# An attention pipeline re-cut into rounds of two steps: matmul pairs in runs of two, three and three

## The chip, the cores and the metric

The kernel runs on one core of a Trainium2 chip. The metric is device time in microseconds, from launch to end. TensorE (PE) multiplies matrices into PSUM (8 banks of 128 x 512 float32), VectorE (DVE), ScalarE (ACT) and GpSimd (POOL) work on elements, SyncE (SP) starts DMAs. The engines run their own instruction streams in order and meet at semaphores.

## The reference

A batch of 4 sequences of 1024 positions with 128 channels goes through a time-mixing layer (projections and a decaying scan), and then through a cell of six attention nodes. The six nodes are nearly all of the time:

```python
for c in range(NUM_NOD):
    nsrc = min(c + 1, MAX_PREV)
    snode = c - nsrc
    eq, ek, ev = (lind + nsrc - 1, lind, lind + nsrc // 2)
    in_q, in_k, in_v = (c - 1, snode, snode + nsrc // 2)
    q = ew[c, 0] * (nodes[in_q] @ We[eq] + be[eq])
    k = ew[c, 1] * (nodes[in_k] @ We[ek] + be[ek])
    v = ew[c, 2] * (nodes[in_v] @ We[ev] + be[ev])
    o = _mha(q, k, v, Wq[c], Wk[c], Wv[c], Wo[c])      # 8 heads of 16 channels, softmax over 1024 keys
    nodes[c] = act_w[c] * o + q
    lind += nsrc
```

## The kernel before

Node and batch entry make a **unit**: 6 x 4 = 24 units, one after the other. A unit is 4 **groups** (4 heads x 512 queries), and a group is 8 **steps** of 128 keys, so there are 768 steps (`STEPS`), 32 per unit (`UC`). In step s TensorE does, for each of the 4 heads of the group:

- a **score** matmul (L540, 50 rows x 128 keys, 512 queries), which writes one of three PSUM banks (`ring`); ScalarE turns it into the exponential in one of 10 slots of `e_ring` (L853). The row maximum is subtracted inside the matmul, by two extra rows of `q_aug`, so the maxima must be known in advance.
- a **maxima** matmul (L566) for the group that comes `LOOKAHEAD` = 14 steps later: 128 queries x 512 keys, into half of one of two double banks (`wide`). Two of them make a **tile** of 128 queries x 1024 keys, which VectorE reduces in one instruction (L1133). There are two tiles in a step, 1536 in all.

Score and maxima matmul use different halves of the array's rows (heads of other parity) and run side by side. Such two are called a **pair** here. After two pairs stands half of a **block**: the exponentials of the step before times the values (L588, four matmuls in the four column groups of the array, 256 query columns each, into the bank `context`). A step is thus pair, pair, half block, pair, pair, half block.

Every unit needs eight **projections** of 128 x 512, which are single matmuls in full width, at fixed steps r = s mod 32: two each for keys (`KH_AT`, L463), output (`OUT_AT`, L491 and L496), values (`V_AT`, L482) and queries (`QH_AT`, L471). In such a step the projection stands in the place of the first half block, and the whole block (512 columns) comes at the step's end. Projections take `ring` banks. ScalarE empties them (L745, L764, L778), for values VectorE does (L998).

Every 8 steps a group of maxima is complete (`finished`); at the start of that step VectorE makes two splits and a transpose of them (L1138, L1142, L1151), and SyncE writes them to DRAM and loads them back into `q_aug`. Every 8 steps ScalarE empties `context` (L868). Once a unit, VectorE takes the reciprocal of the denominators (L1074).

Ahead of step 0 come the time mixing and 14 steps with maxima alone, with filler matmuls (L426); the last 14 steps have no maxima. In the first units some of the time mixing (`MIX_AT`) still runs beside the attention.

Everything is ordered by hand: each engine's program walks over the same steps, and the places of all else are tables of step numbers.

## Time and profile before

| | |
|---|---|
| median of 3 runs | 2265.6 us (2264.27, 2265.6, 2288.34) |
| profiled execution | 2265.8 us, of which the span of the trace 2264.0 us |
| TensorE busy | 2231.4 us (99%) |
| VectorE busy | 2055.1 us (91%) |
| ScalarE busy | 1829.0 us (81%) |
| GpSimd busy | 529.3 us (23%) |
| granted TensorE clock | 0.998 of full |

Times on a line of a trace are start and duration in microseconds from the start of the span. A line with x2 or more merges neighbours: its duration runs from the start of the first to the end of the last. PEld is the weight load that belongs to a matmul, PE the matmul itself. "idle before <-" names how long the engine stood and what let it go.

### The profile page before, as it was taken

To read this page: it belongs to the slowest core of one execution; us is meant where nothing else is said; L and a number is where in the kernel's file an instruction comes from. 1 tells how busy PE (TensorE), PEld (TensorE's weight loads), DVE (VectorE), ACT (ScalarE), POOL (GpSimd) and SP (SyncE) were. 2 spreads that over 40 slices of the span, in tenths; PEclk is the share of its full clock that TensorE was granted. 3 is DMA by queue.
4 is the path that set the end of the run, shared out by engine and by line. 5 is a ranking of instruction groups with operands and counts; after the bars stand their busy time and mean duration, and the time that the engine had idled before them with its cause. 6 is when DMAs were issued, how large, how long until landed. Compare 5 with 4: busy or idle time off the path is not lost.

```text
span 2264.0 us, 46280 instructions
## 1 busy us (share of the span) xinstructions
PE 2231.4 (99%) x17991; PEld 848.7 (37%) x17991; DVE 2055.1 (91%) x2254; ACT 1829.0 (81%) x3431; POOL 529.3 (23%) x667
## 2 busy tenths in 40 slices
PE   7999999999999999999999999999999999999997
PEld 3533333333333333333333333333333333333332
DVE  6989999999999999999998999999999999989995
ACT  4277888888888888888888888888888888888886
POOL 4431230221312202202112112122022022321313
PEclk9999999999999999999999999999999999999999
DMA  4230332422313314224223233133132242241301
GB/s 126 64 72 25 81 71 49 89 64 66 80 46 91 71 33 92 60 61 85 64 57 81 55 69 80 36 78 80 34 82 62 49 85 54 61 95 42 74 25 53
DMA packets 87546, 149.55 MB, mean 66 GB/s; under 512 B 35147, under 2 KB 49951, under 8 KB 87327
## 3 DMA queue, kind: packets, MB, share of 16 engines
q0 software_dynamic: 28224, 94.13, 19.2%
q1 hardware_dynamic: 59102, 52.46, 9.2%
q8 instruction: 142, 2.33, 0.4%
q14 instruction: 78, 0.63, 0.1%
HBM read 42.36 MB, written 14.91 MB: 25 GB/s over the span
## 4 chain that ended last, share of the span: by engine, by line
PE 95%; DVE 2%; issue 1%; ACT 1%; SPq 0%; POOL 0%; DMA 0%; POOLq 0%; ACTq 0%; DVEq 0%
PE ring L540 43%; PE context L588 36%; PE ring L482 2%; PE ring L471 2%; PE ring L463 2%; PE ring L491 2%; PE ring L496 2%; PE wide L566 2%; DVE max_neg L1133 1%; PE context L426 1%; PE ring L369 0%; ACT e_ring L853 0%; PE ring L394 0%; PE ring L391 0%; PE ring L405 0%
## 5 line engine op out<-in xcount | busy, mean ns | idle before, releaser
L1133 DVE TENSOR_REDUCE max_neg<-wide 128x1 f32<-128x1024 f32 x1536 | 1850.4, 1220 | 142.2 <-PE wide L566 136.4
L853 ACT ACTIVATE e_ring<-ring 128x512 f32<-128x512 f32 x3052 | 1658.2, 597 | 286.6 <-PE ring L540 147.6
L566 PE MATMUL wide<-k_aug,q_aug 48*128 48x512 f32 x3072 | 1121.3, 444 | 2.3 <-DVE max_neg L1133 1.4
L540 PE MATMUL ring<-q_aug,k_aug 50*128 50x512 f32 x3052 | 1114.1, 444 | 0.0
L588 PE MATMUL context<-e_ring,v_aug 128*32 128x256 f32 (+1 forms) x10664 | 938.4, 424 | 1.8 <-ACT raw L868 1.6
L540 PEld LDWEIGHTS ring<-q_aug,k_aug 50*128 50x128 f32 x3052 | 455.7, 184 | 749.7 <-ACT e_ring L853 550.3
L566 PEld LDWEIGHTS wide<-k_aug,q_aug 48*128 48x128 f32 x3072 | 457.9, 184 | 12.9 <-issue 6.5
L588 PEld LDWEIGHTS context<-e_ring,v_aug 128*32 128x32 f32 x10664 | 209.9, 107 | 477.0 <-issue 340.9
L342 POOL DMA_DIRECT2D src<-node_dram x40 | 22.9, 572 | 633.2 <-PE ring L482 633.2
L1233 POOL CAST q_part<-q_part 128x512 fp32r<-128x512 f32 x46 | 28.1, 611 | 476.7 <-ACT q_part L778 302.0
L312 POOL DMA_DIRECT2D q_aug<-q_part x138 | 72.1, 522 | 126.3 <-PE ring L540 126.3
L1190 POOL TENSOR_TENSOR rstd<-vareps,neg_half 128x4 f32<-128x4 f32 x24 | 26.9, 1122 | 219.6 <-DVE vareps L897 219.4
L1259 POOL TENSOR_TENSOR ctxT<-ctxT,rden_bc 128x1024 f32<-128x1024 f32 x23 | 54.7, 2377 | 92.3 <-DMA rden_bc<-rden_dram 92.3
L312 POOL DMA_DIRECT2D k_aug<-k_part x138 | 70.0, 514 | 15.1 <-PE ring L540 9.8
L745 ACT ACTIVATE node_ring<-ring,col 128x512 f32<-128x512 f32 x47 | 32.3, 688 | 48.7 <-PE ring L496 40.8
L1235 POOL TENSOR_TENSOR k_part<-k_part 128x512 f32<-128x512 f32 x47 | 60.3, 1283 | 4.9 <-DVE src L902 1.2
L1235 POOL TENSOR_TENSOR q_part<-q_part 128x512 f32<-128x512 f32 x47 | 60.2, 1281 | 4.0 <-POOL k_part L1235 0.2
L868 ACT ACTIVATE raw<-context 128x512 f32<-128x512 f32 x96 | 58.0, 604 | 0.8 <-PE context L588 0.8
L471 PE MATMUL ring<-node_ring,w_q 128*128 128x512 f32 x92 | 51.8, 645 | 0.1
L491 PE MATMUL ring<-node_ring,w_edge_q 128*128 128x512 f32 x92 | 51.8, 644 | 0.0
L1233 POOL CAST k_part<-k_part 128x512 fp32r<-128x512 f32 x46 | 28.3, 615 | 82.9 <-ACT k_part L764 47.5
L496 PE MATMUL ring<-ctxT,w_o 128*128 128x512 f32 x92 | 47.0, 592 | 0.0
(241 smaller groups left out, 890.8 us busy)
## 6 DMA issues: line engine op xcount, KB each, us to landing
q_aug<-q_part POOLq DMA_DIRECT2D x138, 256.0 KB, 4.5
k_aug<-k_part POOLq DMA_DIRECT2D x138, 256.0 KB, 7.1
src<-node_dram POOLq DMA_DIRECT2D x40, 512.0 KB, 7.2
ctxT<-raw SPq DMA_DIRECT2D x380, 32.0 KB, 2.0
rden_bc<-rden_dram SPq DMA_DIRECT2D x23, 512.0 KB
node_dram<-node_ring SPq DMA_DIRECT2D x16, 512.0 KB, 2.9
...
```

The costliest lines, as they stand in the source:

```text
L312: e.dma_start(aug[first + slot:first + SPLIT:len(slots), u % 2, :, :], part[parity:P:2, slots[slot], :]).then_inc(signal, DMA)
L471: e.matmul(bk[:, :], w_q[:, c, :], node_ring[:, b, c % 2, half_of(hf)], start=True, stop=True).then_inc(p_qh, 1)
L491: e.matmul(bk[:, :], w_edge_q[:, c, :], node_ring[:, b, c % 2, half_of(hf)], start=True, stop=False)
L496: e.matmul(bk[:, :], w_o[:, c, :], ctxT[:, half_of(hf)], start=False, stop=True).then_inc(p_o, 1)
L540: e.matmul(bk[:, :], k_aug[first:first + AUG, u % 2, h // 2, chunk * P:(chunk + 1) * P].bitcast(F32R), q_aug[first:first + AUG, u % 2, h / ...
L566: done = e.matmul(wide[w % 2][:, half_of(kh)], q_aug[first:first + SPLIT, u % 2, h // 2, q0:q0 + P].bitcast(F32R), k_aug[first:first + SPL ...
L588: done = e.matmul(bank[CTX_BANK][j * VW:(j + 1) * VW, columns], v_aug[:, u % 2, chunk, hg * HG + j, :], e_ring[:, (HG * z + order_of(z).in ...
L853: e.activation(e_ring[:, n % E_SLOTS, :], bank[where["st", n]][:, :], ACT.Exp, scale=EXP_SCALE).then_inc(a_exp, 1)
L868: e.activation(raw[:, G % 2, :], bank[CTX_BANK][:, :], ACT.Copy).then_inc(a_cv, 1)
L1133: e.tensor_reduce(max_neg[:, G % 2, row:row + 1], wide[w % 2][:, :], AX_X, ALU.max, negate=True).then_inc(v_mx, 1)
L1233: step(e.tensor_copy(high.bitcast(F32R), x))
L1235: signal(e.tensor_tensor(x, x, high, ALU.subtract), signal_to)
```

## The change

Steps are now taken in **rounds** of two (s even, s + 1). The eight pairs of a round stand in runs of two, three and three instead of four runs of two, and three blocks stand between them instead of four half blocks:

- a round without a projection: 2 pairs, half block (second half of step s - 2), 3 pairs, whole block (step s - 1), 3 pairs, half block (first half of step s);
- with a projection, and no middle form: the same, with the projection between the third run and the last half block. This is so where a group begins (s a multiple of 8);
- the **middle form**, in the other rounds with one projection (s mod 8 = 4): 2 pairs, two half blocks in a row, 3 pairs, the projection alone, 3 pairs, two half blocks in a row.

With it go these: the two double banks for the maxima become a ring of four single banks (`MAX_BANKS`), of which projections now take the next one in turn as well; each maxima matmul waits for its own bank and signals for itself; from tile 88 on (`SPLIT_FROM`) every second tile is reduced in two instructions of 512 columns, and so is every tile whose two banks aren't neighbours (`in_halves`: 955 of the 1536 tiles by the tables of the changed kernel). The halves are joined by a minimum when a group is complete, one more small VectorE instruction. ScalarE waits for a free `e_ring` slot once in a step, before its third exponential, and not twice. `LOOKAHEAD` is 12. The projections for queries move by a step, the turning of a final node stands in one round, and the last projection of all is cut in two halves.

By the tables of the changed kernel there are 378 rounds: 193 without a projection, 95 with projections at the end, and 90 of the middle form (23 with keys, 23 with output, 23 with values, 21 with queries).

```diff
--- before.py
+++ after.py
-LOOKAHEAD = 14
+LOOKAHEAD = 12
 E_SLOTS = 10
+MAX_BANKS = 4
...
-        wide = [ctx.enter_context(nc.psum_tensor(f"wide{i}", [P, S], F32)) for i in range(2)]
+        wide = ctx.enter_context(nc.psum_tensor("wide", [P, MAX_BANKS, BANK], F32))
         context = ctx.enter_context(nc.psum_tensor("context", [P, BANK], F32))
-        bank = ([t[:, :] for t in ring] + [t[:, k * BANK:(k + 1) * BANK] for t in wide for k in range(2)] + [context[:, :]])
-        WIDE_BANKS, CTX_BANK = ((3, 4), (5, 6)), 7
+        bank = ([t[:, :] for t in ring] + [wide[:, k, :] for k in range(MAX_BANKS)] + [context[:, :]])
+        MAX_BANK0, CTX_BANK = 3, 7
+        LAST_DEN_BANK, LAST_FILL_BANK = 3, 5
...
-        KH_AT, OUT_AT, TURN_AT, V_AT, QH_AT = (5, 9), (13, 17), (18, 19), (21, 25), (30, UC + 1)
+        K_AT, OUT_AT, TURN_AT, V_AT, Q_AT = (5, 9), (13, 17), 19, (21, 25), (29, UC + 1)
...
+        def products(s):
+
+            u, r = divmod(s, UC)
+            nxt, prev = u + 1, u - 1
+            found = []
+            if 1 <= nxt < UNITS:
+                found += [("k", nxt, hf) for hf in range(2) if r == K_AT[hf]]
+                found += [("v", nxt, hf) for hf in range(2) if r == V_AT[hf]]
+            for unit in (nxt, nxt + 1):
+                if 1 <= unit < UNITS:
+                    found += [("q", unit, hf) for hf in range(2) if s == q_steps(unit)[0][hf]]
+            if 0 <= prev < LAST:
+                found += [("out", prev, hf) for hf in range(2) if r == OUT_AT[hf]]
+                if CELLS[prev][0] == NODES - 1 and r == TURN_AT:
+                    found += [("turn", prev, hf) for hf in range(2)]
+            return found
...
+        SPLIT_FROM = 2 * (UC + LOOKAHEAD)
+
+        def in_middle(s):
+
+            kinds = [kind for kind, _, _ in products(s + 1)]
+            return kinds in (["k"], ["v"], ["q"], ["out"]) and s % NCH != 0
+
+        MAX_BANK_OF, taken = [], 0
+        for s in range(-LOOKAHEAD, ALONE):
+            for k in range(HG):
+                MAX_BANK_OF.append(MAX_BANK0 + taken % MAX_BANKS)
+                taken += 1
+                if s > 0 and s % 2 == 1 and k == (0 if in_middle(s - 1) else HG - 1):
+                    taken += len(products(s))
+
+        def in_halves(w):
+
+            return w >= SPLIT_FROM and w % 2 == 0 or MAX_BANK_OF[2 * w] + 1 != MAX_BANK_OF[2 * w + 1]
+
+        MAXIMA_UP_TO = []
+        for w in range(GROUPS * TILES):
+            before = MAXIMA_UP_TO[-1] if w else 0
+            MAXIMA_UP_TO += [before + 1, before + 2] if in_halves(w) else [before + 1, before + 1]
...
-            def maxima(w, kh):
+            def maxima(h):
+                w, kh = divmod(h, 2)
                 G, t = divmod(w, TILES)
                 u, g = divmod(G, GPU)
                 hg, qh = divmod(g, NHALF)
                 hj, qt = max_tile(t)
-                h = hg * HG + hj
-                first = (h % 2) * ROWS
+                head = hg * HG + hj
+                first = (head % 2) * ROWS
                 q0 = qh * BANK + qt * P
-                if kh == 0:
-                    if w >= 2:
-                        e.wait_ge(v_mx, w - 1)
-                    else:
-                        for i in WIDE_BANKS[w]:
-                            free_bank(i)
+                i = next_max_bank()
+                bk = free_bank(i)
+                freed[i] = (v_mx, MAXIMA_UP_TO[h])
                 if t == 0 and g == 0 and kh == 0 and u > 0:
                     e.wait_ge(d_q, DMA * Q_MOVES * u)
                     e.wait_ge(d_k, DMA * K_MOVES * u)
                 if u == 0 and qh == 0 and t % (2 * CPB) == 0 and kh == 0:
-                    pair = h // 2
+                    pair = head // 2
                     e.wait_ge(d_q0[pair], DMA * Q_MOVES)
                     e.wait_ge(d_k0[pair], DMA * K_MOVES)
-                done = e.matmul(wide[w % 2][:, half_of(kh)], q_aug[first:first + SPLIT, u % 2, h // 2, q0:q0 + P].bitcast(F32R),
-                                k_aug[first:first + SPLIT, u % 2, h // 2, half_of(kh)].bitcast(F32R), start=True, stop=True)
-                if kh == 1:
-                    done.then_inc(p_mx, 1)
+                e.matmul(bk[:, :], q_aug[first:first + SPLIT, u % 2, head // 2, q0:q0 + P].bitcast(F32R),
+                         k_aug[first:first + SPLIT, u % 2, head // 2, half_of(kh)].bitcast(F32R), start=True, stop=True
+                         ).then_inc(p_mx, 1)
...
+            def pair(s, k):
+                scores(s, k)
+                h = HG * (s + LOOKAHEAD) + k
+                if h < 2 * GROUPS * TILES:
+                    maxima(h)
+
+            def product(kind, unit, hf):
+                make = {"k": head_k, "q": head_q, "v": project_v, "out": project_out, "turn": final_turn}[kind]
+                make(unit, hf, next_max_bank())
...
+            for s in range(0, ALONE, 2):
+                pair(s, 0)
+                pair(s, 1)
+                middle = in_middle(s)
+                if s > 0:
+                    weighted(s - 2, second_half, False, True)
+                if middle:
+                    weighted(s - 1, first_half, True, False)
+                pair(s, 2)
+                pair(s, 3)
+                pair(s + 1, 0)
+                if middle:
+                    for kind, unit, hf in products(s + 1):
+                        product(kind, unit, hf)
+                elif s > 0:
+                    weighted(s - 1, whole, True, True)
+                mix_at(s)
+                pair(s + 1, 1)
+                pair(s + 1, 2)
+                pair(s + 1, 3)
+                if middle:
+                    weighted(s - 1, second_half, False, True)
+                else:
+                    for kind, unit, hf in products(s + 1):
+                        product(kind, unit, hf)
+                weighted(s, first_half, True, False)
+                mix_at(s + 1)
...
-                        if n >= E_SLOTS and (n - E_SLOTS) % HG in (0, 2):
-                            e.wait_ge(p_ctx, (n - E_SLOTS) // HG + 1)
...
+                if n >= E_SLOTS and (n - E_SLOTS) % HG == 0:
+                    e.wait_ge(p_ctx, (n - E_SLOTS) // HG + 1)
...
+            for s in range(0, ALONE, 2):
+                for k in range(HG):
+                    exponential(s, k)
+                exponential(s + 1, 0)
+                if s > 0 and s % NCH == 0:
+                    evict_context(s // NCH - 1)
+                if in_middle(s):
+                    for kind, unit, hf in products(s + 1):
+                        evict(kind, unit, hf)
+                mix_at(s)
+                for k in range(1, HG):
+                    exponential(s + 1, k)
+                if not in_middle(s):
+                    for kind, unit, hf in products(s + 1):
+                        evict(kind, unit, hf)
+                mix_at(s + 1)
...
+                first, second = (MAX_BANK_OF[2 * w + kh] - MAX_BANK0 for kh in range(2))
                 if t == 0 and G >= 2:
                     e.wait_ge(v_cmb, G - 1)
-                e.wait_ge(p_mx, w + 1)
-                e.tensor_reduce(max_neg[:, G % 2, row:row + 1], wide[w % 2][:, :], AX_X, ALU.max, negate=True).then_inc(v_mx, 1)
+                if in_halves(w):
+                    for kh, b in enumerate((first, second)):
+                        e.wait_ge(p_mx, 2 * w + kh + 1)
+                        e.tensor_reduce(max_neg[:, G % 2, kh, row:row + 1], wide[:, b, :], AX_X, ALU.max, negate=True).then_inc(v_mx, 1)
+                else:
+                    e.wait_ge(p_mx, 2 * w + 2)
+                    e.tensor_reduce(max_neg[:, G % 2, :, row], wide[:, first:second + 1, :], AX_X, ALU.max, negate=True
+                                    ).then_inc(v_mx, 1)
 
             def split_high(G):
-                e.wait_ge(v_mx, TILES * (G + 1))
-                both = max_neg[:, G % 2, :].rearrange("p (o t) -> p o t", o=2)
-                step(e.tensor_tensor(max_part[:, G % 2, :, 0, :].bitcast(F32R), both, both, ALU.max))
+                e.wait_ge(v_mx, MAXIMA_UP_TO[2 * TILES * (G + 1) - 1])
+                one, two = (max_neg[:, G % 2, kh, :].rearrange("p (o t) -> p o t", o=2) for kh in range(2))
+                e.tensor_tensor(max_all[:, G % 2, :, :], one, two, ALU.min)
+                step(e.tensor_tensor(max_part[:, G % 2, :, 0, :].bitcast(F32R), one, two, ALU.min))
...
+                    if half == 1 and s >= 0:
+                        for odd in (s, s + 1):
+                            if odd % 2 == 1 and in_middle(odd - 1) == (odd != s):
+                                for kind, unit, hf in products(odd):
+                                    if kind == "v":
+                                        evict_v(unit, hf)
```

On TensorE, the two steps with a projection for keys, before, from the half block ahead of that projection's step on (L540 and L566 are a pair, L463 the projection, L588 the block):

```order
L588 MATMUL context<-e_ring,v_aug 32x256 x4
L540 MATMUL ring<-q_aug,k_aug 128x512
L566 MATMUL wide<-k_aug,q_aug 128x512
L540 MATMUL ring<-q_aug,k_aug 128x512
L566 MATMUL wide<-k_aug,q_aug 128x512
L463 MATMUL ring<-src,w_k_fold 128x512
L540 MATMUL ring<-q_aug,k_aug 128x512
L566 MATMUL wide<-k_aug,q_aug 128x512
L540 MATMUL ring<-q_aug,k_aug 128x512
L566 MATMUL wide<-k_aug,q_aug 128x512
L588 MATMUL context<-e_ring,v_aug 32x512 x4
```

The same place in the changed kernel, a round of the middle form (L607 and L631 are a pair, L514 the projection, L652 the block), from its first block on; a third pair and a row like the first follow:

```order
L652 MATMUL context<-e_ring,v_aug 32x256 x8
L607 MATMUL ring<-q_aug,k_aug 128x512
L631 MATMUL wide<-k_aug,q_aug 128x512
L607 MATMUL ring<-q_aug,k_aug 128x512
L631 MATMUL wide<-k_aug,q_aug 128x512
L607 MATMUL ring<-q_aug,k_aug 128x512
L631 MATMUL wide<-k_aug,q_aug 128x512
L514 MATMUL wide<-src,w_k_fold 128x512
L607 MATMUL ring<-q_aug,k_aug 128x512
L631 MATMUL wide<-k_aug,q_aug 128x512
L607 MATMUL ring<-q_aug,k_aug 128x512
L631 MATMUL wide<-k_aug,q_aug 128x512
```

The projection has moved from a `ring` bank into a `wide` bank, and its neighbours on both sides are three pairs.

On VectorE, from one projection for values to the next maxima group, before:

```order
L998 TENSOR_TENSOR v_aug<-ring,v_bias 128x32x16 [waits d_bias_in,p_v,p_ctx]
L1133 TENSOR_REDUCE max_neg<-wide 128x1 [waits p_mx]
L1138 TENSOR_TENSOR max_part<-max_neg 128x2x8 [waits v_mx]
L1142 TENSOR_TENSOR max_part<-max_neg,max_part 128x2x8 [waits v_own]
L1151 STREAM_TRANSPOSE max_turn<-max_part 128x32 [waits v_cmb,d_rows0]
L1133 TENSOR_REDUCE max_neg<-wide 128x1 [waits p_mx,v_cmb]
L1133 TENSOR_REDUCE max_neg<-wide 128x1 [waits p_mx] x15
```

The same engine at the start of a round of the middle form with a projection for values, in the changed kernel (L1254 reduces 512 columns, L1257 a whole tile, L1102 is the old L998):

```order
L1263 TENSOR_TENSOR max_all<-max_neg 128x16 [waits v_mx]
L1264 TENSOR_TENSOR max_part<-max_neg 128x2x8
L1268 TENSOR_TENSOR max_part<-max_all,max_part 128x2x8 [waits v_own]
L1276 STREAM_TRANSPOSE max_turn<-max_part 128x32 [waits v_cmb,d_rows1]
L1254 TENSOR_REDUCE max_neg<-wide 128x1 [waits p_mx,v_cmb]
L1254 TENSOR_REDUCE max_neg<-wide 128x1 [waits p_mx]
L1257 TENSOR_REDUCE max_neg<-wide 128x2 [waits p_mx]
L1102 TENSOR_TENSOR v_aug<-wide,v_bias 128x32x16 [waits d_bias_in,p_v,p_ctx]
L1254 TENSOR_REDUCE max_neg<-wide 128x1 [waits p_mx] x20
```

The four small instructions of a finished group now stand ahead of the tiles of a round that has a projection in its middle; before, they stood in a step without one.

## Rows read from the trace of the kernel before

**Rows 1.** The page: busy us, share of the span, instructions

```profile
PE 2231.4 (99%) x17991; PEld 848.7 (37%) x17991; DVE 2055.1 (91%) x2254; ACT 1829.0 (81%) x3431; POOL 529.3 (23%) x667
```

**Rows 2.** Timeline of TensorE and its weight loads: one half of a step

```profile
1873.48 0.49 PE L540 MATMUL ring<-q_aug,k_aug 50*128 50x512 f32 x1
...
1873.59 0.19 PEld L540 LDWEIGHTS ring<-q_aug,k_aug 50*128 50x128 f32 x1
...
1873.82 0.39 PE L540 MATMUL ring<-q_aug,k_aug 50*128 50x512 f32 x1
...
1874.14 0.64 PE L588 MATMUL context<-e_ring,v_aug 128*32 128x256 f32 x8
...
1874.71 0.49 PE L540 MATMUL ring<-q_aug,k_aug 50*128 50x512 f32 x1
```

**Rows 3.** The same timeline, all engines, at a projection and a finished group

```profile
1877.83 1.16 PE L482 MATMUL ring<-w_v_fold,src 128*128 128x128 f32 x8
...
1878.92 0.50 PE L540 MATMUL ring<-q_aug,k_aug 50*128 50x512 f32 x1
...
1879.11 0.68 DVE L998 TENSOR_TENSOR v_aug<-ring,v_bias 128x512 f32<-128x512 f32 x1
1879.26 0.39 PE L540 MATMUL ring<-q_aug,k_aug 50*128 50x512 f32 x1
...
1879.51 1.09 ACT L853 ACTIVATE e_ring<-ring 128x512 f32<-128x512 f32 x2 [0.43 <-PE ring L540]
1879.58 1.06 PE L588 MATMUL context<-e_ring,v_aug 128*32 128x512 f32 x8
1879.72 1.23 DVE L1133 TENSOR_REDUCE max_neg<-wide 128x1 f32<-128x1024 f32 x1
...
1880.57 0.50 PE L540 MATMUL ring<-q_aug,k_aug 50*128 50x512 f32 x1
...
1881.60 3.46 DVE L1133 TENSOR_REDUCE max_neg<-wide 128x1 f32<-128x1024 f32 x3
```

**Rows 4.** The chain that ended last: fillers and maxima before step 0, a projection

```profile
98.87 0.66 PE wide L566 x2
99.53 0.63 PE context L426 x2
...
1030.04 1.05 PE ring L463 x2
```

**Rows 5.** Timeline of TensorE: a projection for the output

```profile
1052.50 1.12 PE L491 MATMUL ring<-node_ring,w_edge_q 128*128 128x512 f32 x2
...
1054.41 0.50 PE L540 MATMUL ring<-q_aug,k_aug 50*128 50x512 f32 x1
```

**Rows 6.** Timeline of ScalarE: the context is emptied, once a group

```profile
1877.50 0.60 ACT L868 ACTIVATE raw<-context 128x512 f32<-128x512 f32 x1
...
1899.04 0.60 ACT L868 ACTIVATE raw<-context 128x512 f32<-128x512 f32 x1
```

**Rows 7.** Timeline of VectorE and TensorE: a maxima bank that is late

```profile
1045.68 3.46 DVE L1133 TENSOR_REDUCE max_neg<-wide 128x1 f32<-128x1024 f32 x3
...
1046.93 0.49 PE L566 MATMUL wide<-k_aug,q_aug 48*128 48x512 f32 x1 [0.51 <-DVE max_neg L1133]
```

**Rows 8.** Timeline of VectorE: the reciprocal of a unit

```profile
1027.56 0.54 DVE L1074 RECIPROCAL rden_pack<-den_pack 128x64 f32<-128x64 f32 x1
1028.02 3.42 DVE L1133 TENSOR_REDUCE max_neg<-wide 128x1 f32<-128x1024 f32 x3
```

**Rows 9.** Timeline of TensorE: blocks in the last steps, which have no maxima

```profile
2220.20 1.06 PE L588 MATMUL context<-e_ring,v_aug 128*32 128x512 f32 x8
...
2222.25 1.06 PE L588 MATMUL context<-e_ring,v_aug 128*32 128x512 f32 x8
```

**Rows 10.** Timeline of the end: last projection, its statistics

```profile
2252.68 1.10 PE L515 MATMUL ring<-raw,w_last 128*128 128x512 f32 x2 [1.69 <-DVE raw L1026]
...
2255.26 0.89 DVE L888 BATCH_NORM_STATS2 stats<-ring 128x6 f32<-128x128 f32 x4 [0.23 <-PE ring L369]
```

282 lines of the change are left out of this document (147 added, 135 removed), and 2 rows, old and new, of the table MIX_AT.

## The prediction

> **What bounds the kernel now.** I read the page first: TensorE is busy 99% of the span, VectorE 91%, ScalarE 81% [rows 1]. Then the timeline inside a step, to see what TensorE's time is made of. A pair starts 0.34 us after the pair ahead of it, the half block 0.32 after the second pair, the next pair 0.57 after the half block: 1.23 for half a step, 4.92 for two steps [rows 2]. Nothing in it waits. A whole block takes 0.99, only 0.42 more than a half one, a projection 1.05, for values 1.09 and for the output 1.91 [rows 3 to 5]. Two steps with a projection take 2.46 + 2 x 0.66 + 1.05 + 0.99 = 5.82 (values 5.86, output 6.68). A group with one projection for values and one for queries comes to 6 x 2.46 + 3.40 + 3.36 = 21.52, and the trace has 21.54 from one emptying of the context to the next [rows 6]. So TensorE's own order explains the time, and the others fit in beside it.
>
> **What the new order takes off TensorE.** The first pair of a run costs more than the second: its row is 0.49 long against 0.39, because its weights load in the open, while the second pair's load begins 0.11 after the first one's start, in its shadow [rows 2]. So a pair inside a run is worth 0.34 - 0.11 = 0.23. The trace has no run of three; its third pair costs from 0.23 (like the second without the exposed load) to 0.34 (the whole distance). I take 0.23, since the second pair's load already lies under the first pair. A run of two is 0.66, a run of three 0.34 + 0.23 + 0.32 = 0.89. Two half blocks in a row I take as one whole block.
>
> - No projection: 0.66 + 0.57 + 0.89 + 0.99 + 0.89 + 0.57 = 4.57, which is 0.35 less.
> - Projection at the end: 5.62, 0.20 less.
> - Middle form: 0.66 + 0.99 + 0.89 + 1.05 + 0.89 + 0.99 = 5.47, 0.35 less.
>
> If nothing waited, that would be 193 x 0.35 + 95 x 0.20 + 90 x 0.35 = 118 us. Most of it is not to be had.
>
> The Trainium skill speaks against the cheap third pair: "TensorE: Matmul & The Clock Gate", The mechanism, says that a weight load overlaps matmuls in flight only where the row groups differ. Here both row groups are at work and the load still begins 0.11 after the pair, so the trace differs from the rule; by the rule the third pair would be 0.34.
>
> **VectorE's share.** Reductions in a row stand (3.46 - 1.23) / 2 = 1.12 apart [rows 3]. Halves of 512 columns aren't in the trace. The nearest is the value projection's emptying, 512 columns, after which the next reduction starts 0.61 later [rows 3]; from below, half of 1.12 is 0.56. I take 0.59, so a tile in two costs 1.18, and a round with two such tiles 4.60, with four (44 of the rounds without projection) 4.72. VectorE is now as long as TensorE's 4.57. In rounds without a projection I take 4.65: 4.60 from VectorE, and some 0.05 because the fifth score of a round needs the bank of the second. ScalarE starts 0.59 after a run's first pair, its exponentials stand 1.09 - 0.60 = 0.49 apart [rows 3], so the second ends at 0.59 + 0.49 + 0.60 = 1.68, and the fifth pair's weights would load at 1.69. Rounds with the projection at the end: 5.65.
>
> **The middle form, step by step.** A finished group adds 1.88 - 1.12 = 0.76 between two reductions [rows 3]; the new minimum is a fourth such instruction (0 to 0.25 by a third of that), I take 0.10, together 0.86. All groups finish ahead of a round of the middle form. In the round before, the fifth tile half can't be reduced before 3.12 + 0.59 = 3.71, so the last tile starts at 3.71 + 0.03 + 0.59 = 4.33, and the first half of the new round at 4.33 + 1.12 + 0.86 - 4.61 = 1.70 after its start. The second follows at 2.29. The projection takes the bank of the second pair. A whole tile gives its bank back 1.25 after the start of its reduction (1045.68 to 1046.93) [rows 7], a half 0.54 sooner, 0.71. So the projection starts at 3.00 and not at 2.54: **0.46 lost**. Behind it, the whole tile (start 2.88) frees the next bank at 4.13, where TensorE would be at 4.05; the eighth pair needs the fifth one's bank, free at 2.88 + 1.12 + 0.71 = 4.71, just in time, but its load is then in the open (0.1). The last two blocks end at 6.14. ScalarE's seventh exponential waits for a slot that only the first of them frees (5.14 + 0.64 + 0.09), ends at 6.5, and the next round's second pair waits 0.15 for it. Sum 6.29 for keys and queries, where the two steps took 5.82.
>
> - Queries: +0.47, 21 times: 10.
> - Keys: the reciprocal stands just ahead, 0.46 more [rows 8] that used to be hidden behind TensorE. +0.93, 23 times: 21.
> - Output: 1.91 hides the rest, but not the late start: 3.00 + 1.91 + 0.89 + 0.99 + 0.15 = 6.94 against 6.68. +0.26, 23 times: 6.
> - Values: VectorE empties them 1.28 after their start (1877.83 to 1879.11) [rows 3], at 4.28, ahead of the fifth pair's half, which starts at 4.89 and frees the bank at 5.60. The eighth pair waits 0.9. 5.60 + 0.43 + 0.99 + 0.15 = 7.17 against 5.86. +1.31, 23 times: 30.
>
> Together +67 us.
>
> **The rest.** Two steps fewer ahead of step 0 save 2 x 2 x (0.66 + 0.63) = 5.2 [rows 4]; in their stead two of the last steps, 2.05 each [rows 9], become two at 2.33: 4.6 saved in all, 0 to 6. The last projection in halves: from its matmul to the statistics there are 2.58 [rows 10], three operations of which the later half is on the path; I take 1, at most 1.3. SyncE: rows of maxima go out four steps ahead of their use, not six, over 9 us, for a store and a load that take about 6 by the spacing that they have now; no wait. GpSimd's splits and moves keep their steps within one, and it is busy 23%.
>
> **Sum.** -193 x 0.27 = -52, +3 for the 44 with four split tiles, -95 x 0.17 = -16, +67, -4.6, -1: **-4 us**, from the profiled 2265.8 (the median is 2265.6) to **2262 us**. Its own range, with 0.1 us a round either way in 90 rounds and half of that in the others, is 2244 to 2280. A measurement of this kernel can tell about 1%, 23 us.
>
> **Rivals.**
>
> 1. *The middle form doesn't wait* (faster). If the finished group's small instructions and the first halves are done by 2.54, rounds of the middle form cost 5.47 + 0.15, 90 x 0.2 saved in place of 67 lost: 2262 - 85 = 2177. With half of the waits gone: 2220. For it: only VectorE's 0.46 stands between the two, and a late last tile in front makes all of it. Against: the bank follows from the tables, and a late bank already costs TensorE 0.51 once before [rows 7]. Chance 0.25.
>
> 2. *Halves are dear* (slower). If halves in a row stand further apart than 0.60, VectorE sets the rounds without projection. Each 0.01 above costs 140 x 0.04 + 44 x 0.08 + 90 x 0.02 = 11 us; from 0.62 to 0.63 the change is slower by 1%, at the 0.69 of a short reduction standing alone (1.23 - 0.54) it would be 2360. For it: each half waits for a semaphore of its own. Against: the 0.61 after the value projection. Chance 0.17. The Trainium skill, "VectorE: DVE Perf Modes", The TRN2 errata, gives 120 cycles beside the elements for a PSUM source: two halves would cost 0.125 more than a whole, 0.66 each, and by that the time would be near 2330; for the whole it gives 1.19, where the trace has 1.12.
>
> 3. *The third pair costs 0.34* (slower). Rounds without projection are then 4.79 + 0.03, those with one at the end 5.84, the middle form about 0.15 shorter in its waits than it is longer in its pairs: 193 x 0.17 + 95 x 0.19 - 13 = +38, 2300. It decides in every run of three. Chance 0.12.
>
> The forecast itself has 0.46. From these: faster by over 1% (under 2243) 0.27, within 1% 0.49, slower 0.24. The range that should hold 8 in 10 cuts the far end of rival 1 and of rival 2: 2195 to 2310.
>
> **What would show it.** In a round without projection the starts of pairs read 0, 0.34, 1.23, 1.57, 1.80, 3.12, and the round is 4.6 to 4.7 long. Halves of reductions follow at 0.59. In rounds of the middle form TensorE stands about 0.46 ahead of the projection, released by VectorE, and 0.9 ahead of the eighth pair behind values; the four groups of a unit, by their emptyings of the context, take about 21.8, 21.9, 23.1 and 21.3 us from its start on (before, by the sums above, 22.4 in the two that have an output projection and 21.5 in the others). If TensorE is still 99% busy in the middle form, the forecast is wrong, to the fast side.

## The result, and the profile after

The changed kernel takes 2412.2 us (median of 4 runs, 2407.4 to 2418.3) beside 2265.9 for the kernel before: ratio 1.062, 95% interval 1.055 to 1.069. The forecast was 2262, its range ended at 2310.

The page of the kernel after, its first part (engine: busy us, share, instructions), the granted clock and the DMA share in 40 slices, and the lines of the chain:

```profile
PE 2273.9 (94%) x17213; PEld 957.0 (40%) x17213; DVE 2077.8 (86%) x3307; ACT 1789.6 (74%) x3432; POOL 529.6 (22%) x667
...
PEclk9989999999999999999999989999999999899899
DMA  4130331331412323313403223223134133132201
...
PE context L652 21%; PE ring L607 21%; DVE max_neg L1257 10%; DMA rows_dram<-max_turn 9%; DVE max_neg L1254 9%; PE wide L631 6%; PE wide L522 2%; PE wide L533 2%; DMA q_aug<-rows_dram 2%; PE wide L514 2%; PE wide L542 1%; PE wide L547 1%; PE context L477 1%; DVE max_part L1268 1%; DVE max_all L1263 1%
```

TensorE was busy 99% of the span and is now busy 94% [rows 1]. 11% of the chain is two small transfers that no row of mine ahead of the prediction spoke of: the rows of maxima on their way to DRAM and back.

**Where the time went.** I read the start of every round off ScalarE's exponentials (8 to a round, the first starts 0.59 behind the round's first pair) and took the median of each round of the unit over 20 units (free: no projection; end and middle: where the round's projection stands; the group ends ahead of r = 4, 12, 20 and 28):

| round (r) | form | before | forecast | after |
|---|---|---|---|---|
| 2, 6, 10, 18, 22, 26 | free | 4.92 | 4.65 | 4.58 to 4.60 |
| 0, 8, 24 | end | 5.85 to 5.87 | 5.65 | 5.65 to 5.69 |
| 4 | middle, keys | 5.83 | 6.75 | 6.62 |
| 12 | middle, output | 6.70 | 6.94 | 7.01 |
| 20 | middle, values | 5.87 | 7.17 | 7.22 |
| 28 | middle, queries | 4.92 (r = 30: 5.83) | 6.29 (4.65) | 6.35 (4.58) |
| **14** | free | 4.92 | 4.65 | **8.70** |
| **16** | end, output | 6.70 | 6.51 | **8.76** |

The medians add up to 93.8 us for a unit, where it took 87.87. With 4.59 and 6.51 in the last two rows, as the free rounds and run e1 below have them, it would be 87.4, so 6.4 us are lost there in the median unit. The loss differs from unit to unit, 0.5 to 9.6 us; against e1, round by round, the two rounds lose 132 us in the 23 units. The emptyings of the context show the same by groups (start, us; one unit, from its start on 21.4, 29.1, 23.4, 21.2, where the prediction named 21.8, 21.9, 23.1 and 21.3):

```profile
1165.88 0.60 ACT L901 ACTIVATE raw<-context 128x512 f32<-128x512 f32 x1
1187.32 0.60 ACT L901 ACTIVATE raw<-context 128x512 f32<-128x512 f32 x1
1216.38 0.60 ACT L901 ACTIVATE raw<-context 128x512 f32<-128x512 f32 x1 [1.20 <-PE context L652]
1239.76 0.60 ACT L901 ACTIVATE raw<-context 128x512 f32<-128x512 f32 x1
1260.96 0.60 ACT L901 ACTIVATE raw<-context 128x512 f32<-128x512 f32 x1
```

**The free round is as forecast.** Timeline of TensorE, the round at r = 18 of unit 11 (x2 takes two matmuls in one row):

```profile
1221.27 0.49 PE L607 MATMUL ring<-q_aug,k_aug 50*128 50x512 f32 x1
...
1221.60 0.39 PE L607 MATMUL ring<-q_aug,k_aug 50*128 50x512 f32 x1
...
1221.84 0.39 PE L607 MATMUL ring<-q_aug,k_aug 50*128 50x512 f32 x1
1222.16 1.06 PE L652 MATMUL context<-e_ring,v_aug 128*32 128x512 f32 x8
1223.15 0.50 PE L607 MATMUL ring<-q_aug,k_aug 50*128 50x512 f32 x1
```

The third pair of a run stands 0.24 behind the second, and the whole block takes 0.99.

**The middle form waits as forecast.** The round with values that follows begins at 1224.62. In time order: the first of the finished group's four small instructions, two halves (1.18, so 0.59 each) and a whole tile, the projection, its emptying by VectorE, and TensorE's eighth pair. Beside them stand the two half blocks in a row (1225.29) and the pair behind them (1226.29): 1.00 apart, as long as a whole block, which the forecast had taken for granted.

```profile
1225.29 1.07 PE L652 MATMUL context<-e_ring,v_aug 128*32 128x256 f32 x16
...
1225.65 0.17 DVE L1263 TENSOR_TENSOR max_all<-max_neg 128x16 f32<-128x16 f32 x1
...
1226.29 0.50 PE L607 MATMUL ring<-q_aug,k_aug 50*128 50x512 f32 x1
...
1226.36 1.26 DVE L1254 TENSOR_REDUCE max_neg<-wide 128x1 f32<-128x512 f32 x2
1227.54 1.22 DVE L1257 TENSOR_REDUCE max_neg<-wide 128x2 f32<-128x1024 f32 x1
...
1227.67 1.16 PE L533 MATMUL wide<-w_v_fold,src 128*128 128x128 f32 x8
...
1228.93 0.69 DVE L1102 TENSOR_TENSOR v_aug<-wide,v_bias 128x512 f32<-128x512 f32 x1 [0.17 <-issue]
...
1230.27 0.18 PEld L631 LDWEIGHTS wide<-k_aug,q_aug 48*128 48x128 f32 x1 [0.94 <-DVE max_neg L1254]
...
1230.27 0.50 PE L631 MATMUL wide<-k_aug,q_aug 48*128 48x512 f32 x1 [0.49 <-DVE max_neg L1254]
```

The first half starts 1.74 after the round (1.70 forecast), the projection 3.05 (3.00). The weight load of the eighth pair waits 0.94 for its bank (0.9).

**What was not forecast.** The timeline of unit 10, r = 11 to 16: what GpSimd and SyncE issue, and TensorE's last matmuls ahead of its wait and first behind it:

```profile
1098.25 3.04 POOL L357 DMA_DIRECT2D k_aug<-k_part  x6 [0.56 <-issue]
1101.28 0.57 POOL L387 DMA_DIRECT2D src<-node_dram  x1
...
1101.51 0.56 SPq L1530 DMA_DIRECT2D rows_dram<-max_turn  x1
...
1110.68 0.64 PE L652 MATMUL context<-e_ring,v_aug 128*32 128x256 f32 x8
...
1113.08 1.26 SPq L1542 DMA_DIRECT2D q_aug<-rows_dram  x2
...
1115.86 0.76 PE L607 MATMUL ring<-q_aug,k_aug 50*128 50x512 f32 x1 [4.54 <-DMA q_aug<-rows_dram]
```

GpSimd issues 1.5 MB of keys and 0.5 MB of node features; 0.2 us later SyncE issues the 16 KB of rows. SyncE may issue their load only once they have landed, 11.6 us later, and TensorE stands 4.54 for it (over the whole trace 71.7 us in 21 waits, 4.7 at most). In the kernel before the same store was issued ahead of the copies, and its load followed in 2 us:

```profile
1045.79 0.54 SPq L1403 DMA_DIRECT2D rows_dram<-max_turn  x1
1047.74 1.29 SPq L1415 DMA_DIRECT2D q_aug<-rows_dram  x2
...
1048.35 3.04 POOL L312 DMA_DIRECT2D k_aug<-k_part  x6 [0.56 <-issue]
```

What counts is which was issued first. In unit 9 of the kernel after, five of the six copies happen to go out behind the store, and the load follows in 2 us:

```profile
1009.73 0.55 POOL L357 DMA_DIRECT2D k_aug<-k_part  x1 [0.85 <-PE ring L607]
...
1012.37 0.56 SPq L1530 DMA_DIRECT2D rows_dram<-max_turn  x1
...
1013.11 2.50 POOL L357 DMA_DIRECT2D k_aug<-k_part  x5 [2.83 <-issue]
...
1014.35 1.26 SPq L1542 DMA_DIRECT2D q_aug<-rows_dram  x2
```

SyncE's waits for the landing of the rows (total, times, longest), first before, then after:

```profile
SPq L1415 <- DMA rows_dram<-max_turn: 142.9, 96, 2.8
```

```profile
SPq L1542 <- DMA rows_dram<-max_turn: 301.5, 76, 11.0
```

And TensorE in stretches of 5 us in the kernel after (stretch, its length, busy of PE, PEld, DVE, ACT, POOL, then granted clock, DMA share, GB/s): it stands still, then has the lower of its two levels, 1.2 in place of 2.4 GHz, for some 7 us. That is the round at r = 16.

```profile
1105.00:1110.00 5.00, 5.00 (x50) 1.97 (x48) 4.42 (x6) 4.49 (x9) 0.00 (x0) 1.00 1.05 150
1110.00:1115.00 5.00, 1.32 (x14) 0.48 (x12) 2.25 (x3) 1.63 (x4) 0.00 (x0) 0.99 0.23 76
1115.00:1120.00 5.00, 4.14 (x22) 1.76 (x26) 1.99 (x3) 2.18 (x5) 0.00 (x0) 0.50 0.02 5
1120.00:1125.00 5.00, 5.00 (x28) 1.50 (x20) 2.95 (x4) 3.08 (x6) 0.00 (x0) 0.83 0.00 0
```

### The profile page after: what moved, and what is told of

Same layout as the page of the kernel before. It is cut to its first block, busy times and chain, and to the rows that moved or that the text cites. A ratio compares the mean times of both kernels' runs of the same rounds, so it can differ in the third digit from the quotient of the medians.

```text
span 2416.5 us, 45010 instructions
## 1 busy us (share of the span) xinstructions
PE 2273.9 (94%) x17213; PEld 957.0 (40%) x17213; DVE 2077.8 (86%) x3307; ACT 1789.6 (74%) x3432; POOL 529.6 (22%) x667
## 4 chain that ended last, share of the span: by engine, by line
PE 61%; DVE 23%; DMA 11%; issue 2%; POOL 1%; SPq 1%; ACT 0%; DVEq 0%; POOLq 0%; ACTq 0%
PE context L652 21%; PE ring L607 21%; DVE max_neg L1257 10%; DMA rows_dram<-max_turn 9%; DVE max_neg L1254 9%; PE wide L631 6%; PE wide L522 2%; PE wide L533 2%; DMA q_aug<-rows_dram 2%; PE wide L514 2%; PE wide L542 1%; PE wide L547 1%; PE context L477 1%; DVE max_part L1268 1%; DVE max_all L1263 1%
## 5 line engine op out<-in xcount | busy, mean ns | idle before, releaser
L892 ACT ACTIVATE e_ring<-ring 128x512 f32<-128x512 f32 x3054 | 1603.6, 600 | 420.8 <-PE ring L607 350.3
L1254 DVE TENSOR_REDUCE max_neg<-wide 128x1 f32<-128x512 f32 x1910 | 1208.2, 682 | 197.1 <-PE wide L631 192.4
L607 PE MATMUL ring<-q_aug,k_aug 50*128 50x512 f32 x3054 | 1074.4, 449 | 73.6 <-DMA q_aug<-rows_dram 71.7
L631 PE MATMUL wide<-k_aug,q_aug 48*128 48x512 f32 x3072 | 1112.8, 455 | 29.4 <-DVE max_neg L1254 18.6
L652 PE MATMUL context<-e_ring,v_aug 128*32 128x256 f32 (+1 forms) x9888 | 911.0, 454 | 0.6 <-ACT raw L901 0.6
L607 PEld LDWEIGHTS ring<-q_aug,k_aug 50*128 50x128 f32 x3054 | 516.8, 191 | 785.6 <-ACT e_ring L892 576.0
L1257 DVE TENSOR_REDUCE max_neg<-wide 128x2 f32<-128x1024 f32 x581 | 705.7, 1219 | 71.1 <-PE wide L631 70.4
L631 PEld LDWEIGHTS wide<-k_aug,q_aug 48*128 48x128 f32 x3072 | 514.3, 190 | 90.1 <-DVE max_neg L1254 58.2
L652 PEld LDWEIGHTS context<-e_ring,v_aug 128*32 128x32 f32 x9888 | 215.4, 109 | 391.7 <-issue 283.1
L820 ACT ACTIVATE node_ring<-wide,col 128x512 f32<-128x512 f32 x47 | 32.4, 688 | 56.1 <-PE wide L547 56.0
L542 PE MATMUL wide<-node_ring,w_edge_q 128*128 128x512 f32 x94 | 56.9, 689 | 2.3
L522 PE MATMUL wide<-node_ring,w_q 128*128 128x512 f32 x96 | 54.2, 651 | 2.8 <-DVE max_neg L1257 0.6
L547 PE MATMUL wide<-ctxT,w_o 128*128 128x512 f32 x94 | 51.6, 632 | 0.0
```

Source lines behind the costliest of these rows:

```text
L522: e.matmul(bk[:, :], w_q[:, c, :], node_ring[:, b, c % 2, half_of(hf)], start=True, stop=True).then_inc(p_qh, 1)
L542: e.matmul(bk[:, :], w_edge_q[:, c, :], node_ring[:, b, c % 2, half_of(hf)], start=True, stop=False)
L547: e.matmul(bk[:, :], w_o[:, c, :], ctxT[:, half_of(hf)], start=False, stop=True).then_inc(p_o, 1)
L607: e.matmul(bk[:, :], k_aug[first:first + AUG, u % 2, h // 2, chunk * P:(chunk + 1) * P].bitcast(F32R), q_aug[first:first + AUG, u % 2, h / ...
L631: e.matmul(bk[:, :], q_aug[first:first + SPLIT, u % 2, head // 2, q0:q0 + P].bitcast(F32R), k_aug[first:first + SPLIT, u % 2, head // 2, h ...
L652: done = e.matmul(bank[CTX_BANK][j * VW:(j + 1) * VW, columns], v_aug[:, u % 2, chunk, hg * HG + j, :], e_ring[:, (HG * z + order_of(z).in ...
```

## The experiments

Two theories. **Collision**: LOOKAHEAD 12 moves the end of a group from s mod 8 = 2 to 4, so at r = 12 the rows go out behind the copies of the keys, which stayed at r = 10 and 11. **Lead**: the rows go out two steps nearer to their use, and four steps of the new order are too short for the way there and back wherever the copies stand. Later the question became what LOOKAHEAD and TensorE's new order are worth, each by itself. Times are medians; the last columns cut the span at the first exponentials of s = 0, 32 and 704 (profiled execution of each).

| kernel | us | ratio, interval | s 0 to 32 | 32 to 704 | 704 to end |
|---|---|---|---|---|---|
| before | 2265.8 | 1 | 104.9 | 1862.6 | 189.2 |
| after | 2412.2 | 1.062 (1.055 to 1.069) | 123.4 | 1986.7 | 205.1 |
| e1 after, late copies | 2284.9 | 1.008 (1.006 to 1.010) | 127.1 | 1863.1 | 192.7 |
| e2 old order, lead 12 | 2513.7 | 1.109 (1.103 to 1.115) | 105.2 | 2093.3 | 223.8 |
| e3 after, fillers | 2380.3 | 1.050 (1.044 to 1.056) | 128.0 | 1942.0 | 198.4 |
| e4 e1, no middle form | 2286.7 | 1.009 (1.006 to 1.011) | 127.2 | 1865.3 | 191.2 |
| e5 e1, unit 0 in old order | 2278.4 | 1.007 (1.005 to 1.009) | 115.9 | 1865.6 | 192.7 |
| e6 e5, values at end | 2259.0 | 0.997 (0.996 to 0.998) | 115.5 | 1848.8 | 189.0 |
| e7 e5, values emptied later | 2261.1 | 0.997 (0.996 to 0.999) | 114.1 | 1847.4 | 193.9 |
| e8 e1, halves from step 0 | 2280.9 | 1.007 (1.006 to 1.008) | 117.0 | 1864.2 | 194.1 |
| e9 after, source load later | 2365.8 | 1.044 (1.042 to 1.045) | 125.1 | 1940.8 | 199.1 |
| e10 e2, store and spread apart | 2396.9 | 1.057 (1.055 to 1.059) | 105.2 | 1992.7 | 209.4 |
| e11 e6, reciprocal later | 2282.4 | 1.008 (1.007 to 1.009) | 115.9 | 1868.0 | 194.5 |
| e12 e10, late copies | 2302.5 | 1.016 (1.014 to 1.017) | 105.2 | 1891.8 | 196.7 |
| e13 after, LOOKAHEAD 14 | 2252.1 | 0.995 (0.993 to 0.997) | 117.0 | 1837.8 | 189.1 |
| e14 e13, unit 0 in old order | 2243.1 | 0.990 (0.989 to 0.991) | 108.9 | 1835.5 | 189.1 |
| e15 e14, values at end | 2224.2 | 0.983 (0.981 to 0.984) | 108.9 | 1813.4 | 188.4 |
| e16 e15, no middle form | 2224.0 | 0.984 (0.981 to 0.987) | 108.9 | 1815.2 | 188.1 |

### e1: the copies of the keys behind the rows

```diff
-                    if r == 10:          # first three copies
+                    if r == 14:
...
-                    if r == 14:          # load of the node features
+                    if r == 15:
...
-                if 1 <= nxt < UNITS and half == 0 and r == 11:   # other three
+                if 1 <= nxt < UNITS and half == 0 and r == 15:
```

> The changed kernel, with one thing moved: GpSimd issues its six copies of the keys (k_aug from k_part) at steps r = 14 and 15 of a unit and not at 10 and 11, and the next load of src one step later. Theory 1 (collision): the rows of maxima, which since LOOKAHEAD = 12 are stored at r = 12, lie on the DMA engines behind these six copies and the load, and TensorE waits for them at r = 16. Then the wait of about 4 us and the low clock behind it go in each of 22 units, 22 x 6.4 = 140 us: 2265 to 2285 us. Theory 2 (lead): a store and a load of the rows don't fit into the four steps, whatever else moves: 2380 us or more.

127 us back. The round at r = 14 takes 4.59, at r = 16 6.51, and SyncE waits 2.5 at most for the store to land:

```profile
SPq L1542 <- DMA rows_dram<-max_turn: 116.0, 76, 2.5
```

The lead is what it was. The collision is shown, and the theory that four steps are too short falls.

### e9: only the node features later

The load of the node features waits for step 17; the copies of the keys stay.

```diff
-                    if r == 14:
+                    if r == 17:
+                        e.wait_ge(p_st, HG * s)
                         load_source(e, nxt, 1)
```

> The kernel after with one transfer moved alone: the load of the node features (512 KB, one DMA of GpSimd's queue), issued right behind the last copies of the keys (6 of 256 KB at r = 10 and 11), waits for step 17. The copies stay where they are. Theory: the 16 KB store of the rows of maxima lands behind everything that GpSimd's queue had been given before it, and the load is a quarter of these 2 MB; at 150 to 190 GB/s it takes about 3 us of the 11. The round at r = 14 comes down from 8.70 to about 5.5 to 6.5, the granted clock then stays up and the round at r = 16 goes from 8.76 to about 6.6: 22 x 4.5 = 100 us off, 2300 to 2340. Rival: only what is in the queue when the store is issued counts by number, or the copies alone fill the time: r = 14 stays above 8.0 and the time above 2380.

It gave 46 us, half of what I expected, and neither theory nor rival had that time: r = 14 went from 8.70 to 7.60, r = 16 from 8.76 to 8.07, the longest wait for the landing from 11.0 to 10.3. The load of the rows is issued 12.5 us behind the first of the copies in place of 13.8 (medians of units 2 to 21). So the copies of the keys by themselves hold the rows back for nearly as long. In seven of the 23 units, where r = 14 took at most 6.7, r = 16 reads 6.5 to 6.6; in the others it reads 8.0 or more.

### e3: matmuls of no use ahead of the round at r = 16

```diff
             for s in range(0, ALONE, 2):
+                if s % UC == 16:
+                    bk = free_bank(ring_turn[0] % 3)
+                    for _ in range(4):
+                        e.matmul(bk[:, :], w_time_t[:, 0, :], w_time_t[:, 0:CPB, :], start=True, stop=True)
                 pair(s, 0)
```

> The changed kernel, with four filler matmuls of 512 columns (3.4 us, result unused) on TensorE ahead of the first pair of step r = 16 in every unit, where it waits for the rows. Theory 3 (clock): of the 6.4 us that a unit loses there, some 4 are the wait and 2.3 the clock of 1.2 GHz behind it, since TensorE stood still. Busy fillers under the wait keep the clock: 2355 to 2380 us, and the wait itself stays. Rival (the clock is not the cause of the slow rounds behind): 2410 to 2430 us.

The rows land nearly as late as before, and the slow round is gone (r = 16: 6.51). That the round at r = 14 takes 8.44 says little by itself: the fillers take 3.6 us there in every unit, most of it under the wait. SyncE's waits show that the delay is still there:

```profile
SPq L1546 <- DMA rows_dram<-max_turn: 286.7, 76, 10.8
```

All stretches of 5 us from 1095 to 1125, where this kernel has the same wait, read 1.00, for example

```profile
1110.00:1115.00 5.00, 5.00 (x44) 2.00 (x42) 3.82 (x7) 3.56 (x7) 0.00 (x0) 1.00 1.06 151
1115.00:1120.00 5.00, 5.00 (x30) 2.09 (x29) 3.44 (x4) 2.83 (x6) 0.00 (x0) 1.00 0.70 149
```

So of the 6.4 us of the median unit some 4.1 (8.70 - 4.59) are the wait and 2.25 (8.76 - 6.51) the clock behind it. The whole gained 32 us, at the short end of what I expected.

### e2, e10, e12: the old order with LOOKAHEAD 12

e2 is the kernel before with LOOKAHEAD 12 and its tables, nothing else.

> The kernel before, with LOOKAHEAD = 12 and the three tables that go with it, and nothing else of the change: no rounds, no single banks. Theory 1 (collision): here too the rows are stored at r = 12, behind the copies of r = 10 and 11, though 11 us and not 9 lie ahead of their use: a wait of 2 to 3 us and about 2 us of low clock in 22 units, 2340 to 2390 us. Rival (the new order of pairs and blocks is what makes the rows late): 2255 to 2265 us, two steps less ahead of step 0.

Missed, in size and place: the loss lies at r = 6 and 8 (9.43 and 10.20 for 4.92 and 5.85), only 0.8 at r = 14. SyncE's queue in e2 (the store of the rows, store and spread of the reciprocals, the load of the rows):

```profile
1112.94 0.60 SPq L1403 DMA_DIRECT2D rows_dram<-max_turn  x1
1113.58 1.28 SPq L1443 DMA_DIRECT2D rden_dram<-rden_pack  x2
1117.36 0.64 SPq L1450 DMA_DIRECT2D rden_bc<-rden_dram  x1
1118.04 1.31 SPq L1415 DMA_DIRECT2D q_aug<-rows_dram  x2
```

The old code stores and spreads the reciprocals in one step; with a group ending at r = 4 too, SyncE waits for that store with the load of the rows behind it. The change had taken the two apart, so I had left out a thing that the change does right. e10 puts it in:

```diff
                         if r == 4:
-                            spread_rden(prev)
+                            store_rden(prev)
+                        if r == 5:
+                            spread_rden(prev)
```

> The kernel before with LOOKAHEAD 12 (as e2, 2513.7 us) and SyncE's store and spread of the reciprocals issued in two steps, r = 4 and r = 5, behind the load of the rows of maxima, as the change has them. Theory head of the queue: e2 lost its time at r = 6 and 8 (9.43 and 10.20 us, 4.92 and 5.85 before), since SyncE stood at the spread, waiting for the store to land, with the load of the rows behind it; with the two apart these rounds are 4.92 and 5.85 again and what is left is the small loss at r = 10 and 14 (1.1 us together): 2265 to 2290. Theory copies: in the old order too the 2 MB of copies delay the rows at r = 14 once these come a step after them: 2350 or more.

r = 6 and 8 are 4.92 and 5.85 again, but r = 14 and 16 now take 7.40 and 9.85. My reading of e2 (a small loss at r = 14) did not carry over. The traces show where it went: in all three kernels the load of the rows is issued 13.8 to 14.0 us behind the first of the copies (medians of units 2 to 21: after 13.8, e10 13.9, e2 13.95), but in e2 the store itself goes out 6.5 us behind that copy, in e10 3.9 and in the kernel after 2.8, so that less of this time is left to wait for. What counts: with nothing of TensorE's new order in it, LOOKAHEAD 12 makes the collision. It costs 131 us here, of which e12 gives 94 back.

```profile
SPq L1415 <- DMA rows_dram<-max_turn: 277.4, 74, 10.8
```

e12 is e10 with e1's edit.

> The kernel of e10 (old order of TensorE, LOOKAHEAD 12, store and spread of the reciprocals apart: 2396.9 us) with the copies of the keys at r = 14 and 15 as in e1. e10 lost at the same two rounds as the kernel after (r = 14: 7.40, r = 16: 9.85), without any of the new order. If the lead and the place of the copies are all there is to it, these rounds are 4.92 and 6.70 again and the two steps saved ahead of step 0 show at last: 2265.8 - 4.6, so 2258 to 2266, and the new order of TensorE taken by itself (e6 with 2259.0, e5 with 2278.4, e1 with 2284.9, all with this lead and these copies) is then worth nothing or less. Rival: something else of lead 12 costs the old order time too, 2275 or more, and the new order would be worth 16 us or more.

The rival was right: 2302.5, 37 above before, with the copies out of the way. r = 4, 12, 20 and 28 take 6.35, 6.94, 6.11 and 5.16 for 5.83, 6.70, 5.87 and 4.92, 1.24 a unit or 27 us. With LOOKAHEAD 12 the finished group's instructions on VectorE stand ahead of these four rounds, also in the old order (three of them have a projection, r = 28 has none there), and the waits of TensorE and its weight loads for VectorE's reductions rise from 6.4 to 20.8 us; that these instructions are the whole of the 27 is a reading and wasn't tried by itself. Some 10 us more lie in units 20 and 22, at r = 28 and 30, and weren't followed further.

### e4, e6, e7: the middle form

e4 is e1 with in_middle returning False: every projection at its round's end.

> As the kernel with the later copies, and no round of the middle form: every projection stands at its round's end. By the prediction's working a round of the middle form is 6.3 to 7.2 us long, since the small instructions of a finished group come just ahead of it on VectorE. At the end form the same delay meets the fifth pair (its bank is free at 2.41, not 1.80) and costs 0.7: 6.4, 6.8 for keys, 7.2 for the output, 6.4 for values. Against the kernel with the later copies 5 to 15 us less. Rival (the lone projection itself makes the middle rounds long): 90 x 0.9, 60 us less or more.

The same as e1, and not 5 to 15 us less. By rounds the middle form takes 0.10 off the keys, 0.32 off the output, 0.11 off the queries and puts 0.72 on the values. e6 (on e5, below) takes the values alone out of it:

```diff
-            return kinds in (["k"], ["v"], ["q"], ["out"]) and s % NCH != 0
+            return kinds in (["k"], ["q"], ["out"]) and s % NCH != 0
```

> The kernel of e5, and the projections of values no longer in the middle form but at the end of their rounds. In e4 the round at r = 20 took 6.50 with the projection at the end, in e1 7.22 in the middle, while those of keys, output and queries were 0.10, 0.32 and 0.11 shorter in the middle. Theory (each round's price stands by itself): 22 x 0.72 = 16 us below e5, so 2247 to 2250 if e5 gives 2263, faster than the kernel before. Rival (the wait goes on to the next round, since VectorE is as long as TensorE): under 5 us below e5.

19 us, as each round's price had said. e7 leaves them in the middle and has VectorE empty them one tile later.

> The kernel of e5, with values in the middle form, but emptied by VectorE one tile later, behind the tile of the fifth and sixth pair instead of ahead of it. If the prediction's step was right that the eighth pair waits 0.9 us for the fifth one's bank, which stands behind the emptying, the round at r = 20 comes down from 7.22 to 6.3 to 6.5 (VectorE's own work there is 4 x 1.18 + 0.86 + 0.6 = 6.2): 15 to 20 us below e5. If VectorE's total sets that round, it stays above 7.0 and the time within 4 us of e5.

r = 20: 6.35 for 7.22; 17 us. So the values' price was the emptying that stands ahead of the fifth pair's half, as the prediction had it.

### e5, e8: unit 0

e1's excess of 19 us lies in the first 32 steps (127.1 for 104.9). There most tiles (53 of 64 by the tables) are reduced whole, and TensorE waits for them: ahead of a matmul up to 2.2 us at a time in e1, never over 0.7 before. e5 runs the 32 steps in the old order.

> The kernel after with the copies of the keys at r = 14 and 15, and with the steps of unit 0 (s < 32) in the old order: two pairs, half block (or projection), two pairs, half or whole block, every step. What is left of the late-copies kernel's excess over the kernel before (2284.9 against 2265.8) lies by the first exponentials in the first 32 steps: 127.1 us there against 104.9 before and 105.2 in the old order with LOOKAHEAD 12; from s = 40 to s = 704 both kernels take 1840 us. Theory order: the new order waits beside the time mixing, whose instructions on VectorE stand between whole tiles; the old order gives the 22 us back: 2260 to 2266. Theory lead: two steps less lead leave the mixing no room whatever the order: 2280 or more. Rival: unit 0 gains but the first rounds of unit 1 start with buffers late: 2270 to 2275.

e8 makes halves there instead (SPLIT_FROM = 2 * LOOKAHEAD).

> The late-copies kernel (e1) with one number changed: tiles are reduced in halves from the ones made in step 0 on, not from those made in step 32 on. In unit 0 a whole tile gives both banks back only 1.25 us after its reduction began, and by the waits of that stretch TensorE stands up to 2.2 us at its pairs for VectorE's whole tiles, with the granted clock at 0.50 for a stretch behind it. Theory banks: halves give the first bank back 0.54 sooner and take over half of the 22 us away: 2268 to 2275. Theory mixing: what is late is VectorE itself, behind the mixing's own instructions, and halves only add 0.06 for each of 32 tiles: 2283 to 2290.

Each takes 10 or 11 of the 22 us off, not 22: 115.9 and 117.0; the whole time falls by 6.6 and 4.0 us, and none of the expectations for the two runs had these times. The old order beside the old banks needs 105.2 (e12). With LOOKAHEAD 14 the old order beside the new banks needs 108.9 (e14, below). So what is left in e5 comes from what it keeps of the change, and is larger with the shorter lead; the projections that take their bank from the four of the maxima are the candidate, and that wasn't tried.

### e11: the reciprocal in another round

```diff
-                    if half == 1 and r == 3:     # VectorE's reciprocals; store, spread, normalise follow
+                    if half == 0 and r == 8:
```

Store and spread of the reciprocals follow at r = 8 and 9 (they were at 4 and 5), GpSimd's normalising at r = 10 (it was at 8).

> The kernel of e6 (2259.0 us) with the reciprocals of the denominators taken by VectorE in step r = 8, a round with the projection at its end, where TensorE has 1 us more than VectorE, in place of r = 3, just ahead of the middle form with the keys; its store, its spread and GpSimd's normalising follow at r = 8, 9 and 10. By the prediction's step the reciprocal costs the round at r = 4 its 0.46: measured 6.62 for keys against 6.35 for queries, so 0.27 of it shows. Theory: r = 4 goes to 6.35, 22 x 0.27 = 6 us below e6, 2251 to 2255. Rival: the normalised context comes late for the output projection at r = 13, and the rounds at r = 12 and 14 grow by more than that: 2260 to 2290.

The keys' round fell to 6.35 as expected, but r = 8 grew by 0.41 and r = 12 by 0.18, once to 11.90, which over all units is 8 and 16 us: TensorE's weight loads now wait 17.2 us in all for the normalised context and its matmuls 3.3; in e6 neither waits for it. 23 us worse. The rival was right.

### e13 to e16: the new order with the old lead

e13 is the kernel after with LOOKAHEAD 14 and its tables, and TURN_AT 17 (a finished node feature's turning, in three units; at 19 it would fall into the last unit's steps without maxima).

> The kernel after with LOOKAHEAD 14 again (and the tables that go with it, and the turning of a finished node feature at r = 17 instead of 19); order, halves, banks and the copies of the keys (r = 10 and 11) as in the change. A finished group now falls ahead of rounds at r mod 8 = 2, which have no projection, and its rows go out a step ahead of the copies, as before. Theory lead: both losses of the change are LOOKAHEAD's. The rounds at r = 14 and 16 read 4.6 and 6.5, the middle form 5.6 to 6.0 (6.7 for the output) since nothing stands between VectorE's tiles there, and the 0.86 of a finished group falls on a round of 4.6, hidden as far as the round has room (none, so up to 5.4). Sum of a unit 83.7 to 87.1 against 87.87 before; with some 20 us lost in unit 0, 2195 to 2265. Theory order: the middle form waits by itself, whatever finishes there; the unit stays at 87 or more, and the time at 2270 to 2290.

> The kernel of e13 with unit 0 in the old order of steps, as in e5. e5 gained 11 us in the first 32 steps over e1 and 6.6 us in all; here as much: 5 to 12 us below e13. If unit 0 was late for lead 12 alone, within 3 us of e13.

> The kernel of e14 with the values' projections at the end of their rounds, as in e6. If their price in the middle (0.72 a round) came from the finished group ahead of them, it is gone with lead 14 and this kernel is the same as e14 or up to 5 us slower; if it came from VectorE's emptying between the tiles, it is 10 to 16 us faster, as e6 was.

> The kernel of e15 (2224.2 us) with no middle form at all: every projection at the end of its round. In e15 the rounds at r = 4 and 28 take 5.95 and 5.91 with keys and queries in the middle, while the rounds at r = 8 and 20, keys and values at the end, take 5.66 and 5.69; the output takes 6.53 in the middle (r = 12) and 6.51 at the end (r = 16). Theory: with the old lead no finished group stands ahead of these rounds, the end form costs them what it costs elsewhere, and 22 x (0.29 + 0.25) = 12 us come off: 2208 to 2216. Rival: as with lead 12 (e4 against e1: nothing either way), 2220 to 2230.

2252.1, as the lead theory had it: 160 us below the kernel after, 13 below before. The rounds at r = 4, 12, 20, 28 take 5.94, 6.53, 6.73 and 5.91, and a group's end in a free round costs nothing at r = 2 and 18, 0.54 at r = 10 and 0.38 at r = 26. e14 gains 9 more in unit 0, e15 19 by the values (r = 20: 5.69 for 6.73), more than the 10 to 16 expected of the emptying between the tiles; e16, without any middle form, is the same as e15: r = 28 gains 0.20, r = 4 loses 0.11, r = 10 loses 0.12. The rival held there. e15's page, its first part:

```profile
PE 2192.7 (98%) x17101; PEld 932.5 (42%) x17101; DVE 2067.7 (92%) x3282; ACT 1786.5 (80%) x3432; POOL 530.3 (24%) x667
```

(e15's profiled execution took 2241.5, 17 above its median; all of it lies ahead of step 0, where the granted clock reads 0.50 from 62 to 110 us and 1.00 in e16's.) By their ratios e15 and e16 are 1.7% and 1.6% faster than the kernel before.

## Why the prediction was wrong

**The step that failed** is the one on the queues: "SyncE: rows of maxima go out four steps ahead of their use, not six, over 9 us, for a store and a load that take about 6 by the spacing that they have now; no wait. GpSimd's splits and moves keep their steps within one". The steps and their lengths are right (r = 12 to 16, some 9 us), and so is that GpSimd's moves keep their steps; "no wait" doesn't follow from them. The spacing was read in a kernel in which the store goes out ahead of the copies (1045.79 and 1048.35), and LOOKAHEAD moves the one and not the other. The time of a transfer was taken for a property of the transfer; it hangs on what was issued ahead of it. From the store to the load's issue it took 11 us, not 2, and the clock fell behind the wait: 6.4 us in the median unit, 132 in the 23 units, where the difference to before is 146. e1 gave 127 back.

**LOOKAHEAD "4.6 saved in all"** was the second miss. With the copies out of the way it costs the old order 37 us (e12). The prediction had part of this price, but booked it to the middle form, whose waits it worked out with "All groups finish ahead of a round of the middle form". That was so only by LOOKAHEAD 12; the way to cut the sum was by lead and order, not by form. Whether the two steps fewer ahead of step 0 saved their 4.6 these traces can't tell: the first exponential comes at 107.2 before, at 101.2 after and at 106.9 in e12, the last two with the same lead.

**What held.** The third pair 0.24 (0.23 forecast), halves 0.59, free rounds 4.59 (4.65), end form 5.65, middle form 6.62, 7.01, 7.22 and 6.35 (6.75, 6.94, 7.17, 6.29). So rival 1 (the middle form doesn't wait), rival 2 (dear halves, 0.62 and more) and rival 3 (0.34) all fell, and the unit without the collision takes 87.4, where the forecasts of its rounds add up to 87.8. (In rival 2 the 140 rounds should be 149, 193 less 44, which leaves its 11 us as they are.) None of the rivals was about a transfer, which is where the slower side lay.

**Unit 0** was left out of the sum. It cost 22 us (e1), in part by whole tiles or the order (each fix took some 10, and the two weren't tried together); the tables of the time mixing were seen to move and not costed.
